# Post-norm transformer with routed experts on one core: the experts' first bias moved from the activation call into PSUM

## The reference, cut to what matters

```
h   = (x - mu) / sqrt(var + eps) * ln_gamma + ln_beta
ew1, ew2 = quant(expert_w1), quant(expert_w2)         # ternary times a scale per row
h1  = silu(einsum('btd,efd->ebtf', h, ew1))           # 8 experts, 512 wide
eo  = einsum('ebtf,edf->ebtd', h1, ew2)
out = x + shared + gate * eo[argmax expert]           # then a layer norm
```

## Time and profile before

| | |
|---|---|
| median of 3 runs | 833.81 us |
| profiled execution | 832.9 us, its span 831.6 us |
| PE busy | 749.8 us, 90% of the span |
| DVE busy | 701.7 us, 84% |
| ACT busy | 662.1 us, 80% |
| POOL busy | 340.9 us, 41% |
| silu of the routed experts, L1904 | 188 calls, 95.1 us |
| their matmuls, L1285 | 752, 76.4 us |

### The profile page before, as it was taken

One profiled execution on the slowest core, in us unless ns is written; L12 is line 12 of the kernel. 1 busy time (PEld: TensorE's weight loads), 2 busy tenths in 40 slices (PEclk: granted clock), 3 DMA queues, 4 the chain that ended last, 5 costly groups with the idle time before them and its releaser, 6 DMA issues.

```text
span 831.6 us, 18563 instructions
## 1 busy us (share of the span) xinstructions
PE 749.8 (90%) x5485; PEld 597.5 (72%) x5485; DVE 701.7 (84%) x2072; ACT 662.1 (80%) x1457; POOL 340.9 (41%) x370
## 2 busy tenths in 40 slices
PE   2789999999999999999999999999675999988872
PEld 1468777787877878888787887887543777777762
DVE  4867877899889889889988988988757799999885
ACT  2456668987997987898799798796744899999994
POOL 3000020133524224243342522337635299886767
PEclk9969999999999999999999999999868999999997
DMA  7113210202222131131213220102114458765430
GB/s 258 27 54 100 76 52 26 84 26 78 71 89 96 53 102 59 55 130 39 78 65 96 90 77 33 51 27 71 58 46 140 122 164 233 211 182 163 148 119 30
DMA packets 50306, 76.50 MB, mean 92 GB/s; under 512 B 8541, under 2 KB 31007, under 8 KB 50208
## 3 DMA queue, kind: packets, MB, share of 16 engines
q1 hardware_dynamic: 39104, 48.42, 20.0%
q0 software_dynamic: 9600, 25.25, 8.4%
q10 hardware_dynamic: 1504, 1.64, 0.6%
HBM read 47.42 MB, written 28.91 MB: 92 GB/s over the span
## 4 chain that ended last, share of the span: by engine, by line
PE 63%; ACT 16%; issue 9%; DVE 5%; POOL 4%; ACTq 1%; DMA 0%; DVEq 0%; POOLq 0%; SPq 0%
PE bank L592 8%; ACT G_S L1904 6%; PE bank L799 6%; PE bank L812 6%; PE bank L672 4%; ACT G_y L1920 3%; PE bank L544 3%; PE bank L674 3%; PE bank L673 3%; PE bank L684 3%; PE bank L620 2%; PE bank L621 2%; ACT G_T L1880 2%; PE bank L604 2%; PE bank L767 2%
## 5 line engine op out<-in xcount | busy, mean ns | idle before, releaser
L3462 POOL TENSOR_TENSOR R<-rstd,mhalf 128x4 f32<-128x4 f32 x16 | 19.5, 1220 | 278.8 <-DVE rstd L1961 278.8
L3633 POOL DMA_INDIRECT out<-G_y,Gid x72 | 83.6, 1161 | 35.4 <-ACT G_y L1920 13.2
L1904 ACT ACTIVATE G_S<-bank,e1b,e1s 128x256 f32<-128x256 f32 (+1 forms) x188 | 95.1, 651 | 2.2 <-PE bank L1285 2.2
L1285 PE MATMUL bank<-G_T,E1T 128*128 128x256 f16 (+1 forms) x752 | 76.4, 251 | 8.0 <-issue 4.4
L592 PE MATMUL bank<-X,PT 128*128 128x257 f32 x320 | 81.0, 392 | 1.1 <-DVE X L2005 0.9
L3506 POOL DMA_INDIRECT rrec<-R,pos x64 | 67.0, 1047 | 29.2 <-issue 20.7
L3497 POOL DMA_INDIRECT hrec<-HN,pos x64 | 65.7, 1027 | 29.0 <-issue 16.0
L1297 PE MATMUL bank<-E2T,G_Sh 128*128 x288 | 65.6, 274 | 9.5 <-DVE G_Sl L3437 9.2
L1285 PEld LDWEIGHTS bank<-G_T,E1T 128*128 x752 | 59.7, 99 | 19.6 <-issue 11.6
L812 PE MATMUL bank<-E2T,Sh 128*128 128x256 f16 x256 | 60.8, 282 | 6.3 <-DVE Sl L2138 6.3
L1297 PE MATMUL bank<-E2T,G_Sl 128*128 x288 | 65.8, 275 | 0.0
(11 more groups left out here) (392 smaller groups left out, 2459.2 us busy)
## 6 DMA issues: line engine op xcount, KB each, us to landing
XT<-in_xT SPq DMA_DIRECT2D x16, 512.0 KB, 3.9
X<-in_x SPq DMA_DIRECT2D x16, 512.0 KB, 5.8
G_h<-hrec SPq DMA_DIRECT2D x25, 257.0 KB, 3.6
G_r<-rrec SPq DMA_DIRECT2D x25, 257.0 KB, 3.5
e1n<-in_ew SPq DMA_DIRECT2D x8, 512.0 KB
e2n<-in_ew SPq DMA_DIRECT2D x8, 512.0 KB, 3.4
G_h<-hrec SPq DMA_DIRECT2D x22, 128.5 KB, 2.1
G_r<-rrec SPq DMA_DIRECT2D x22, 128.5 KB, 2.3
```

The source lines that it names most:

```text
L1285: last = pe.matmul(bk[:, o + a:o + b], E1T[:, e, c, ff * P:(ff + 1) * P], gt[:, x, c, a:b], start=k == 0, stop=k == 3)
L1904: last = act.activation(G_S[w % NGS][:, ff, a:b], bk[:, o + a:o + b], ACT.Silu, bias=e1b[:, e, ff], scale=e1s[:, e, ff])
L3633: pool.indirect_dma_start(t["out"], bass.IndirectOffsetOnAxis(Gid[w % NGI][:, j:j + 1], 0), G_y[w % NGY][:, j, :], None, bounds_check=TOK ...
```

## The change

The bias is no longer an operand of silu. Once, before the routed experts begin, the raw bias of all 8 x 4 = 32 expert-chunks (without the scale, since silu's scale is applied to the sum) is split in three bf16 parts, laid side by side (`zb3`, 128 x 96), transposed by PE (`bias_rows`) and copied to `ZBT` (96 x 128, `bias_copy`). `pick` is a 96 x 32 matrix of zeros and ones: column (e, f) selects the three parts of bias (e, f). In each chunk a new first matmul takes `ZBT` as stationary operand and the one column of `pick`, repeated over all 256 or 128 columns, as moving operand; it writes the bias into PSUM, and the four matmuls of before add to it. Silu then reads a scale by pointer and an immediate 0 as bias.

```diff
+    zb3 = sb("zb3", [P, 3, NE * FC], BF16)
+    ZBT = sb("ZBT", [3 * NE * FC, P], BF16)
+    pick = sb("pick", [3 * NE * FC, NE, FC], BF16)
 ...
+        def bias_rows():                                    # PE
+            pe.wait_ge(s["zb"], NZB)
+            pe.wait_ge(s["TTl"], at("TTl", B - 1, 1))
+            pe.transpose(banks[3][:].bitcast(BF16)[0:3 * NE * FC, 0:P], zb3[:].rearrange("p k q -> p (k q)"), identb[:]).then_inc(s["zbT"], 1)
 ...
         hT(14, 1)
+        bias_rows()
         logits(14)
 ...
                 for a, b, e in [...]:
+                    pe.matmul(bk[:, o + a:o + b], ZBT[:], pick[:, e, ff].to_broadcast([3 * NE * FC, b - a]), start=True, stop=False)
                     for k, (x, c) in enumerate([(x, c) for x in range(2) for c in range(DC)]):
                         last = pe.matmul(bk[:, o + a:o + b], E1T[:, e, c, ff * P:(ff + 1) * P],
-                                         gt[:, x, c, a:b], start=k == 0, stop=k == 3)
+                                         gt[:, x, c, a:b], start=False, stop=k == 3)
 ...
-                    last = act.activation(G_S[w % NGS][:, ff, a:b], bk[:, o + a:o + b], ACT.Silu, bias=e1b[:, e, ff], scale=e1s[:, e, ff])
+                    last = act.activation(G_S[w % NGS][:, ff, a:b], bk[:, o + a:o + b], ACT.Silu, scale=e1s[:, e, ff])
 ...
+            elif w == 0:
+                ins = dve.tensor_tensor(e1b[:, es], e1b[:, es], e1s[:, es], ALU.mult)
             else:
-                ins = dve.tensor_tensor(e1b[:, es], e1b[:, es], e1s[:, es], ALU.mult)
+                ins = dve.tensor_copy(zb3[:, 0], zb)
 ...
+        def bias(k):                                        # DVE
+            if k >= 1:
+                dve.wait_ge(s["zb"], k)
+            n = NE * FC
+            if k == 0:
+                dve.wait_ge(s["guard"], 20)
+                dve.tensor_tensor(pick..., identb[0:3 * n, 0:n], identb[0:3 * n, n:2 * n], ALU.add)
+                ins = dve.tensor_tensor(zb, zb, zb3[:, 0], ALU.subtract)
+            elif k == 1:
+                dve.tensor_tensor(pick..., pick..., identb[0:3 * n, 2 * n:3 * n], ALU.add)
+                ins = dve.tensor_copy(zb3[:, 1], zb)
+            else:
+                ins = dve.tensor_tensor(zb3[:, 2], zb, zb3[:, 1], ALU.subtract)
+            ins.then_inc(s["zb"], 1)
+
+        def bias_copy():
+            dve.wait_ge(s["zbT"], 1)
+            dve.tensor_copy(ZBT[:], banks[3][:].bitcast(BF16)[0:3 * NE * FC, 0:P]).then_inc(s["zbc"], 1)
 ...
         r(12, 1)
+        for i in range(NZB):                                # NZB = 3
+            bias(i)
         ode(7, 8)
 ...
             router(14, i)
+        bias_copy()
         place(14, 0)
```

More of the change, by code:

```diff
@@ L320, in program @@
         "ode nb gn1 gn2 nb2 osum gnr oexp oexp2 "
-        "bn0 bng mv0 mvg ve0 ve1 ve2 veg rs1 rs2 rsg csum bias padrow wqk bqk w0l "
+        "zb zbT zbc bn0 bng mv0 mvg ve0 ve1 ve2 veg rs1 rs2 rsg csum bias padrow wqk bqk w0l "
         "counts sort mixed "
@@ L1275, in gup @@
             elif f0 == 0:
+                pe.wait_ge(s["zbc"], 1)
                 pe.wait_ge(s["sort"], NSORT)
@@ L2458, in guard @@
                 ins = dve.tensor_reduce(e1b[:, es], bk[:, 0:2 * FC * n].rearrange("p (e f two) -> p e f two", f=FC, two=2), AX.X, ALU.add)
+            elif w == 0:
+                ins = dve.tensor_tensor(e1b[:, es], e1b[:, es], e1s[:, es], ALU.mult)
             else:
-                ins = dve.tensor_tensor(e1b[:, es], e1b[:, es], e1s[:, es], ALU.mult)
+                ins = dve.tensor_copy(zb3[:, 0], zb)
             ins.then_inc(s["guard"], 1)
+        zb = e1b[:, 0:NE].rearrange("p e f -> p (e f)")
+        def bias(k):
[4 more added lines that the diff above has]
+                dve.wait_ge(s["guard"], 20)
+                dve.tensor_tensor(pick[:].rearrange("k e f -> k (e f)"), identb[0:3 * n, 0:n], identb[0:3 * n, n:2 * n], ALU.add)
+                ins = dve.tensor_tensor(zb, zb, zb3[:, 0], ALU.subtract)
+            elif k == 1:
+                dve.tensor_tensor(pick[:].rearrange("k e f -> k (e f)"), pick[:].rearrange("k e f -> k (e f)"), identb[0:3 * n, 2 * n:3 * n], ALU.add)
+                ins = dve.tensor_copy(zb3[:, 1], zb)
[5 more added lines that the diff above has]
+            dve.tensor_copy(ZBT[:], banks[3][:].bitcast(BF16)[0:3 * NE * FC, 0:P]).then_inc(s["zbc"], 1)
         def rest(k):
@@ L3640, in pool_program @@
             gid_(w - 2)
-    NCONST, NREST, NSORT, NMIX = 7, 50, 10, 10
+    NCONST, NREST, NSORT, NMIX, NZB = 7, 50, 10, 10, 3
     sp_program()
```

## The result

The changed kernel takes 837.5 us (median of 20 executions, 835.6 to 840.1), the kernel before 833.55 us beside it (20 executions): ratio 1.0048, 95% interval 1.0038 to 1.0059, so 4.0 us slower (3.2 to 4.9). A second measurement in a later session, in which both kernels were slower, gave 1.0071 (1.0044 to 1.0097). The forecast was 836.6 us, slower. The profiled execution took 837.2 us with a span of 835.9.

The account below looks back on a forecast made before the run. ACT bounds the kernel, DVE and PE close behind, PE's sequencer next in paired groups. Full groups 0, paired +2.65, preparation +0.2 give +2.85 us: 835.7 profiled, 836.6 median; range 835 to 838, 8 in 10 within 832.5 to 840.

Parts of the forecast that it names:

- Silu without a pointer: ACT's 188 silu calls: each 0.09 us shorter without the bias pointer, 16.9 us together, 0.36 per full group, 0.72 per paired.
- Rival E: Silu calls get no shorter; paired groups still go at PE's 5.75 us and the total is 837 us; chance 0.03.
- D: ACT bounds throughout, so all 16.9 us saved on silu's pointers come through: 817 us; chance 0.03.
- One sign: Expected in the trace if the forecast was right: ACT busy below 95% in the full groups.
- Full groups, 0 forecast: Full-group iterations: PE rises from 4.04 to 4.50 us, near the mean of 4.53, so no net change (-2 to +1.5).
- Rival C: Full groups are hit too, 4.62 us an iteration against 4.53, +2.0 us, total 838.7 us; chance 0.15.
- A step of the sequencer, 0.125 forecast: Paired groups: eight more register operations on PE's sequencer cost 1.0 us, so an iteration goes from 4.75 to 5.75 us.
- A: Paired groups: added register operations are hidden behind the second product, ACT's 4.78 us sets the pace: 829.9 us; chance 0.12.
- B: Paired groups: a register step costs only about 0.08 us, so no change overall, 833.4 us; chance 0.17.
- The end, -1.85 forecast: After the last first product: ACT lags 1.75 us instead of 3.2 (-1.5), and the last four silu calls are shorter (-0.35).
- The preparation, +0.2 forecast: Before the routed experts: five added DVE instructions stick out of an idle gap by 0.2 us (0 to 0.6); the rest is hidden.
- the 2.65 of the sum: Net loss of the paired groups in us: +4.5 for slower iterations, less 1.5 and 0.35 regained at the end.

Follow-up runs that it names:

- no_product: Changed kernel without its added bias matmuls, silu still without a bias pointer, so this bias is missing from the result: 0.9931 of the kernel before.
- no_scatter: no_product, and also without the indirect stores of the full groups' results and the waits for them: 0.9855 of the kernel before.
- fixed_column: Changed kernel with every added matmul taking expert 0's column at a fixed address, so without their register operations: 0.9956 of the kernel before.
- tables: Changed kernel with selection columns put in group order once, so fixed addresses, and one 256-column product for two in paired groups: 0.9950 of the kernel before.
- double_product: Changed kernel with a second added matmul, of zeros and with the same register address, behind each one in the paired groups: 1.0051 of the kernel before.
- paired_only: Kernel before with the preparation and the change in paired groups alone; full groups read the scaled bias by pointer: 1.0015 of the kernel before.
- after_again: The changed kernel, unaltered, measured again in a later session: 1.0071 of the kernel before.
- prep_only: Changed kernel with the preparation but no added matmuls; silu reads the scaled bias by pointer from a new tile: 0.9956 of the kernel before.
- prep_again: prep_only measured once more, on another chip: 0.9979 of the kernel before.

## Why the prediction was right

- **Silu without a pointer.** 0.45 to 0.36 and 0.34 to 0.25: the 0.09 of the prediction, as measured and as the Trainium skill ("ScalarE: Activation LUTs", "What ACT_TABLE_LOAD costs", about 93 ns) has it. Rival E is out as far as the calls go, D is out since without the product the full groups gained nothing (no_product). One sign missed by a hair: ACT is busy 38.02 of 40 us in the full groups, 95.05%, not below 95%.
- **Full groups, 0 forecast, 0 measured** (4.51 and 4.51). The size of PE's part was a little off: 4.38 clean instead of 4.50, since the 4.04 from which I started held 0.11 of waiting (an iteration that waits for nothing takes 3.93 in the traces of before and of no_product); the four products cost 0.45, 0.46 forecast. The reason given was incomplete: I named three engines, and no_product and no_scatter show that the loads of `G_h` were the limit and DVE the next one. The two equal means hide a change: with the product 17 of the 22 iterations take 4.38 to 4.44, PE's own pace, and five are held up to 5.04; before they were spread from 3.93 to 5.59. That the means agree to 0.01 is luck. Rival C didn't happen, though single iterations rose to 5.0 when a load was late (700.77 follows 695.79 in PE's starts).
- **A step of the sequencer, 0.125 forecast.** Twelve starts from 779.3 to 780.8 have 11 intervals, 0.136 each; the chunks of the second half, three steps each, follow each other by 0.375, which is 0.125 a step. The nine iterations from the wait to the last first product took 51.6 us (765.72 to 817.33), 51.5 forecast. fixed_column ties some 70% of the loss against no_product to the register operations, and tables and double_product agree. The sum put all of it there; the rest, 0.24 of 0.8 to 0.9 us a group, stays with the matmuls when the register operations are gone. Rivals A and B fail here; so does the back-to-back figure of 81 ns of the Trainium skill ("TensorE: Matmul & The Clock Gate", "Back-to-back issue gap") as a price for these steps: the matmuls take 0.056 and the steps 0.125.
- **The end, -1.85 forecast.** Last first product to last silu: 1.43 us (817.33 to 818.76) instead of 3.2, and 1.01 for the four calls instead of 1.37: -2.15. The twelve register steps of 0.125 that the prediction put there did not set the pace: the first matmuls of this half follow each other by 0.28 to 0.29 a chunk, the matmuls' own pace, since the sequencer had run ahead during the second product (its register operations for them start at 816.4).
- **The preparation, +0.2 forecast.** Too much. DVE's timeline, which answers to the earlier trace rows:

```profile
578.68 0.17 DVE L2485 TENSOR_TENSOR pick<-identb 96x32 bf16<-96x32 bf16 x1
...
579.28 0.19 DVE L2491 TENSOR_TENSOR zb<-e1b,zb 128x32 bf16<-128x32 f32 x1
579.39 0.25 DVE L2218 TENSOR_TENSOR o_T<-bank,W1x 128x96 f32<-128x96 f32 x1
```

Five instructions in 0.7 us fit into the idle gap: the step behind them starts at 579.39 instead of 579.46. Counted from the step for `R` ahead of them (577.89 and 578.03) it starts 1.50 us later instead of 1.43, so 0.07 sticks out. As a whole, though, the kernels with the preparation alone came out 1.8 to 3.7 us below before, which no term of the sum has.

What the sum lacked: it gave +2.8 and the runs show +4.0 and +6.0. In the profiled pair the part from the first full iteration to the last norm call (655.2 to 827.7 against 653.7 to 823.4) is 2.8 us longer, near the 2.65 of the sum; over the whole routed part it is 3.1, and 3.8 to 3.9 in paired_only and after_again. So the routed part was forecast 0.2 to 1.2 too short. The rest stood already at its beginning, behind a stretch in which the clock of the changed kernel was 0.77 (575 to 590 us) and that of before 1.00. That clock does not come with the preparation or the tiles' places: fixed_column has both unchanged and was at 1.00 there. Yet its routed part begins as late (638.2 against 638.3, and 637.1 before), so the clock alone doesn't explain the late start.

That the total came so near is in part luck. Against prep_only and prep_again, which have the preparation and no product, the changed kernel is 0.92% slower both times, 7.7 us, and the traces of both pairs show only 3.4 of it in the routed part. Ahead of it they show 3.2 in one pair and 0.7 in the other, where the sum has +0.2 for the preparation. These 4 us stay open, as the 1 to 3 us of the tiles do.

What before was limited by is seen better afterwards: the 0.75 that the prediction called ACT's reserve over the sequencer was the whole gain on offer, no_product took 0.3 of it per iteration and some of it at the end, and the change spent it and 0.5 more.

## What to carry to other kernels

Before a matmul is added to free another engine, look at PE's sequencer and not only at PE: where operands are addressed by registers and the matmuls are short (128 columns), the count of register operations sets the pace, at 0.12 us each here, and a matmul that reuses an address cost next to nothing beside it (0.04 us for eight). With fixed addresses eight of them still cost 0.24 us. If a choice by data has to be made in such a loop, make it once outside (a table in the order of the loop) and keep the loop's addresses static. And where three limits lie within 3% of each other, neither a gain nor a cost on one of them moves the time: find by leaving work out which of them holds, here first the loads, then DVE. And have a kernel with the preparation alone beside the changed one: here it moved the zero by as much as the effect.

## What the runs showed of the hardware

- A register operation with the weight load and matmuls behind it takes 0.125 us on PE's sequencer, whether one product or one to three expert matmuls follow (chunks of three operations 0.375 us apart from 779.91 to 780.66); in this program two matmuls in a row with the same register address share one operation (double_product).
- Reading an expert number into a register of PE's sequencer takes 0.30 us (TENSOR_LOAD, 296 to 319 ns), and some 0.7 us from one to the next (777.9, 778.6, and the register operations of the second half from 779.3).
- Declaring tiles that nothing uses, which moves others, came out at 0.9978 of before (0.9955 to 1.0001), an interval that just includes no change; a change of 0.2 to 0.4% that moves tiles needs such a kernel beside it.
- The granted clock of the 10 us around one and the same 2.0 us wait of PE was 0.83 in one execution and 1.00 in another, and between them in others.
- The same kernel took 834.2 us in one session and 848.4 and 849.0 in later ones. There is no later trace of it, but the two traces of the changed kernel place the difference: its routed part takes 197.6 and 198.4 us and begins at 638.3 and 651.4. The ratio between two kernels can differ too (1.0048 and 1.0071), though the intervals overlap.
